# Second attention of a two-layer Flamingo block: transposed scores, row maxima from a first pass, fp32 value products

## The chip, the cores and the metric

One core of a Trainium2 chip runs the whole program: one launch, all inputs in HBM at the start, the output in HBM at the end. The metric is device time in microseconds; lower is better. A core has five engines that run their own programs and wait for each other through semaphores: TensorE (PE, matmuls into PSUM), VectorE (DVE), ScalarE (ACT), GpSimd (POOL) and SyncE (SP), which here only starts DMAs.

## What is computed

X (4 batches, 512 positions, 512 features) goes through two layers, each a cross attention and a feed-forward net, each added to X with a gate. The fourth of five stages is the attention of the second layer, and the change is there:

```python
def xattn(q, k, v):              # 4 batches, width 512 split into 8 heads of 64 rows (ch = 64)
    attn = einsum('bct,bcs->bts', q * ch**-0.5, k * ch**-0.5)   # per head 512 x 512
    attn = softmax(attn, axis=-1)
    return einsum('bts,bcs->bct', attn, v)
# q = layernorm(X), k = v = ctx_2048; X += tanh(g_xattn[1]) * result
```

The width is the second axis of X (512 rows, 64 of them a head), and the queries t and the keys s are its last axis. So in memory a head is 64 partitions, two heads make a tile of 128, and queries and keys are its 512 columns.

## The kernel before

The program has five stages one after the other, with a barrier between: `mlstm_phase`, `spline_phase`, `ffn0_phase`, `attention_phase`, `ffn1_phase`. Each stage is written as one program for each engine; the order on an engine is the order of the code, and every `wait_ge` blocks all that stands behind it on the same engine. No planner is at work.

`attention_phase` goes through the 4 batches. At the start of a batch (`norm`, `split`) VectorE takes the maximum of ctx, GpSimd spreads it over partitions (L1770), VectorE normalises X into XN and ScalarE and VectorE split keys, queries and values into a high and a low fp16 part (KH/KL, QH/QL, VH/VL), so that three fp16 products stand for one fp32 product. TensorE turns ctx for the values (L1868).

Then come 32 units in a row, one for each head (8) and each block of 128 queries (4). A unit is:

- `scores` (L1832): three fp16 matmuls, 128 queries by 512 keys, into one of three PSUM banks. The keys of a head stand in 128 rows of which 64 are zero, so that all 128 rows of the array are used.
- `top` (L1944, L1946): VectorE takes the row maximum, negates and scales it.
- exponential (L1805): ScalarE with that as bias, and with the row sum as a second output.
- `turn` (L1840): four fp32 transposes of the probabilities, 128 x 128 each.
- `high`, `low` (L1792, L1950): ScalarE and VectorE split the turned probabilities into fp16 parts.
- `weigh` (L1852): twelve fp16 matmuls of 64 columns.
- `scale` (L1798): ScalarE multiplies by the inverse sum (L1955) into OT.

Every eighth unit `back` turns a finished block (L1860) and VectorE adds it into X (L1960). TensorE's order in the loop is scores of unit u + 2, turn of u, weigh of u - 2. The three pairs of weights of the next stage (W1H, W1L) are loaded here by SyncE, one pair at each of the first three batches (L1749).

`ffn1_phase` runs 16 tiles of 128 rows; the gate and up products of a tile (L2084) use W index 0 and 1, the down products (L2110) index 2, and they begin two tiles later.

Of the kernel before, what the change touches and what calls it, by code (L numbers as in the profile page):

```python
# [1699 lines left out]

def attention_phase(nc, A, X, tg, idf, store, WH1, WL1, stack):


    def sb(name, shape, dt=F32):
# [21 lines left out]
    RS = sb("RS2", [P, NC])  # L1726
    EPS = sb("EPS2", [P, 1])
    CM = sb("CM2", [P, 8])
    SB = [stack.enter_context(nc.psum_tensor(f"A_S{i}", [P, 512], F32)) for i in range(3)]
    PB = [stack.enter_context(nc.psum_tensor(f"A_P{i}", [P, 512], F32)) for i in range(2)]  # L1730
    OB = [stack.enter_context(nc.psum_tensor(f"A_O{i}", [P, 512], F32)) for i in range(2)]
    TB = stack.enter_context(nc.psum_tensor("A_T", [P, 512], F32))
    (ctx_loaded, mv_ready, sd_ready, xn_ready, t_ready, t_taken, s_ready, max_ready, p_ready, pt_ready, ph_ready,
     pl_ready, o_ready, ot_ready, own_sem, passed, pre_ready, cm_ready, cm_all, cs_ready, vh_ready,
     vl_ready, kh_ready, kl_ready, qh_ready, ql_ready, rc_ready, norm_own) = (sem("d_" + n) for n in (
         "ctx", "mv", "sd", "xn", "t", "t_taken", "s", "max", "p", "pt", "ph", "pl", "o", "ot", "own", "passed", "pre", "cm", "cm_all", "cs", "vh", "vl", "kh", "kl", "qh", "ql", "rc", "norm_own"))
# [606 lines left out]
```

## Time and profile before

| what | value |
|---|---|
| median of 3 runs | 1674.55 us (1672.92 to 1677.72) |
| profiled execution, own time | 1677.74 us |
| its span | 1676.0 us |
| mean granted clock of TensorE | 0.901 |
| TensorE busy | 1346.0 us |
| VectorE busy | 1241.5 us |
| ScalarE busy | 767.8 us |
| GpSimd busy | 325.5 us |

Busy time is the union of an engine's instructions. The span is that of one profiled execution; its own time lies 1.7 us above. A matmul's length in a row covers its way through the array, so that the distance of two starts, and not the length, is what one costs in a stream. The granted clock is a share of full speed: 1.0 is 2.4 GHz and 0.5 is 1.2 GHz; a mean between the two is a mixture of both.

### The profile page before, as it was taken

The numbers are of one execution on the slowest core, as the hardware profiler recorded it, in microseconds if no ns is written. First come the engines' busy times: TensorE is split into PE (matmuls) and PEld (weight loads), VectorE is DVE, ScalarE is ACT, GpSimd is POOL, SyncE is SP. The second block draws the span as 40 slices with busy tenths as digits, with TensorE's granted clock in tenths as the row PEclk, the third lists the DMA queues.
The fourth block names the chain that finished last, engine by engine and source line by source line (L and its number), as shares of the span: only waits on it lengthen the run. The fifth ranks groups of instructions, "written<-read, shape, count | busy, mean of one in ns | idle before, by whom it ended". The sixth has DMA issues, their size and how long they took to land. (4 is left out here: it accounts for less than half of the span.)

```text
span 1676.0 us, 24635 instructions
## 1 busy us (share of the span) xinstructions
PE 1346.0 (80%) x8976; PEld 758.8 (45%) x9000; DVE 1241.5 (74%) x1952; ACT 767.8 (46%) x1451; POOL 325.5 (19%) x233
## 2 busy tenths in 40 slices
PE   5599993636868989873967759679999999999996
PEld 3378773212334444432645546334444444444443
DVE  5567777825558778956999999488877777887764
ACT  3445562715334444424978879323333334433322
POOL 0032424607445557531000000000000000000000
PEclk8789996558888999996979889789999999999998
DMA  8312231355142242226030000000000000000000
GB/s 290 117 52 61 102 101 41 128 147 157 55 131 83 90 124 88 101 67 247 3 125 0 25 0 0 1 1 7 6 6 13 6 6 6 6 6 9 10 6 13
DMA packets 56493, 102.17 MB, mean 61 GB/s; under 512 B 9823, under 2 KB 20727, under 8 KB 56300
## 3 DMA queue, kind: packets, MB, share of 16 engines
q1 hardware_dynamic: 55148, 97.14, 17.5%
q0 software_dynamic: 1280, 4.20, 0.9%
q8 instruction: 37, 0.61, 0.2%
q14 instruction: 28, 0.23, 0.0%
HBM read 73.47 MB, written 27.66 MB: 60 GB/s over the span
## 5 line engine op out<-in xcount | busy, mean ns | idle before, releaser
L2084 PE MATMUL HG<-W1H,XT 128*128 128x512 f16 x512 | 166.6, 387 | 27.2 <-ACT XT L2045 20.7
L1558 PE MATMUL FD<-W0D,HH 128*128 128x512 f16 x512 | 159.6, 395 | 14.8 <-DMA W0D<-down_weights,IDX 12.2
L2084 PE MATMUL HU<-W1H,XT 128*128 128x512 f16 x512 | 163.2, 380 | 0.0
L2110 PE MATMUL HD<-W1H,HT 128*128 128x512 f16 x512 | 155.2, 380 | 0.0
L1552 PE MATMUL FG<-F,W0G 97*128 97x512 f16 x324 | 86.1, 400 | 52.9 <-DMA F<-features_kept 24.5
L2053 ACT ACTIVATE SG<-HG,DS 128x512 f32<-128x512 f32 x64 | 43.9, 686 | 160.6 <-PE HU L2084 160.6
L1805 ACT ACTIVATE PR<-A_S,NM,CM 128x512 f32<-128x512 f32 x128 | 99.5, 777 | 34.2 <-DVE NM L1946 34.2
L2187 DVE SCALAR_TENSOR_TENSOR H<-HU,DS,SG 128x512 f32<-128x512 f32 x64 | 48.0, 750 | 87.6 <-ACT SG L2053 85.7
L1442 POOL TENSOR_TENSOR HL<-HM,HH 128x512 f16<-128x512 f32 x64 | 92.3, 1442 | 86.0 <-ACT HH L1481 85.5
L335 ACT ACTIVATE DD<-E,TM 128x128 f32<-128x128 f32 x256 | 72.7, 369 | 70.3 <-PE E L431 68.7
L1558 PE MATMUL FD<-W0D,HL 128*128 128x512 f16 x256 | 100.1, 391 | 0.0
L2084 PE MATMUL HG<-W1L,XT 128*128 128x512 f16 x256 | 99.1, 387 | 0.0
L2110 PE MATMUL HD<-W1L,HT 128*128 128x512 f16 x256 | 97.2, 380 | 0.0
L2084 PE MATMUL HU<-W1L,XT 128*128 128x512 f16 x256 | 97.2, 380 | 0.0
L1481 ACT CAST HH<-HM 128x512 f16<-128x512 f32 x64 | 39.6, 618 | 120.4 <-DVE HM L1645 120.4
L1944 DVE TENSOR_REDUCE NM<-A_S 128x1 f32<-128x512 f32 x128 | 86.3, 674 | 8.3 <-PE A_S L1832 8.3
L1832 PE MATMUL A_S<-KH,QH 128*128 128x512 f16 x128 | 52.1, 407 | 49.9 <-DVE VL L1939 49.9
L2084 PEld LDWEIGHTS HG<-W1H,XT 128*128 128x128 f16 x512 | 50.8, 99 | 91.2 <-DVE H L2187 27.7
L1950 DVE SCALAR_TENSOR_TENSOR PL<-A_P,PH 128x512 f16<-128x512 f32 x128 | 87.9, 686 | 5.2 <-ACT PH L1792 4.8
L2062 ACT CAST HQ<-V 128x2048 f16<-128x2048 f32 x16 | 30.4, 1898 | 128.4 <-DVEq L2209 128.4
L1840 PE MATMUL A_P<-CST,PR 128*128 128x128 f32 x512 | 83.2, 286 | 6.9 <-ACT PR L1805 6.3
L1645 DVE SCALAR_TENSOR_TENSOR HM<-FG,DS,SG 128x512 f32<-128x512 f32 x54 | 40.5, 750 | 64.5 <-PE FG L1552 35.4
(335 smaller groups left out, 3369.8 us busy)
## 6 DMA issues: line engine op xcount, KB each, us to landing
VALP<-in_ffn_weights_dram SPq DMA_DIRECT2D x24, 512.0 KB, 3.6
VALQ<-in_ffn_weights_dram SPq DMA_DIRECT2D x24, 512.0 KB, 3.6
quantised_weights<-QQ SPq DMA_DIRECT2D x24, 512.0 KB, 2.8
X<-in_x_dram SPq DMA_DIRECT2D x8, 1024.0 KB, 6.0
CTX<-in_ctx_dram SPq DMA_DIRECT2D x8, 1024.0 KB, 5.6
W1H<-quantised_weights SPq DMA_DIRECT2D x3, 2048.0 KB, 10.6
W1L<-quantised_weights SPq DMA_DIRECT2D x3, 2048.0 KB, 15.4
F<-features_kept SPq DMA_DIRECT2D x16, 288.0 KB
```

What stands on the lines that cost most here:

```text
L335: ins = nc.scalar.activation(DD[:, n % 4, c * P:(c + 1) * P], E[n % 2][:, c * P:(c + 1) * P], ACT.Exp, bias=TM[:, 13 + c, b, h:h + 1])
L1442: pool.tensor_tensor(HL[:, i, :], HM[:, i % 2, :], HH[:, i, :], ALU.subtract).then_inc(hl_ready, 1)
L1552: last = pe.matmul(banks[t][:, :], GW[rows, t, lhs, cols], F[b % 2][rows, rhs, c, :], start=(n == 0), stop=(n == 2))
L1558: last = pe.matmul(DN[c][:, :], lhs[:, i, c * P:(c + 1) * P], W2[:, i, part, :], start=(i == 0 and n == 0), stop=(i == KI - 1 and n == 2))
L1805: nc.scalar.activation(PR[:, u % 2, :], SB[u % 3][:, :], ACT.Exp, bias=NM[:, 1, u:u + 1], scale=CM[:, 5:6], accum_out=SM[:, u:u + 1]).then ...
L1832: last = pe.matmul(SB[u % 3][:, :], lhs[:, c, cols], rhs[:, c, par, :], start=(i == 0), stop=(i == 2))
L1840: last = pe.transpose(PB[u % 2][:, k * P:(k + 1) * P], PR[:, u % 2, k * P:(k + 1) * P], idf)
L1944: own.inc(v.tensor_reduce(NM[:, 0, u:u + 1], SB[u % 3][:, :], AX.X, ALU.max, negate=True))
L1950: v.scalar_tensor_tensor(out=PL[:, u % 3, :], in0=PB[u % 2][:, :], scalar=XS, in1=PH[:, u % 3, :], op0=ALU.mult, op1=ALU.subtract).then_in ...
L2084: ins = pe.matmul(bank[:, :], lhs, rhs, start=(i == 0), stop=(i == len(terms) - 1))
L2110: ins = pe.matmul(DN[0][:, :], HT[:, q, lp, k, :], W[:, 2, i * D:(i + 1) * D], start=(i == 0 and lp == 0 and W is WH), stop=(i == KI - 1 a ...
L2187: v.scalar_tensor_tensor(out=H[:, i * 512:(i + 1) * 512], in0=U[i % 2][:, :], scalar=DS[:, 1:2], in1=SG[:, i % 2, :], op0=ALU.mult, op1=AL ...
```

## The change

The whole of `attention_phase` is written anew; the loops over batches are unrolled.

- A step is now two heads (the two halves of 128 partitions), one block of 128 keys, and all 512 queries: 64 steps, `STEPS_A`. Eight steps (two pairs of heads) are a quad. The scores come out transposed, keys in partitions, so the turn of the probabilities, their split and the turn back of the result are gone.
- `scores(k)`: six fp16 matmuls with 64 contraction rows (two heads, in different halves of the array's rows, into different PSUM banks), and one more for each head with two contraction rows, a row of ones against the negated maxima of the queries (`MB`, as a bf16 pair).
- These maxima come from a first pass one quad ahead: `largest(g, i)` multiplies only the high parts, 128 queries by 512 keys for two heads, into the one buffer `MX`; VectorE's `slot(g, i)` reduces it with one instruction. Eight slots make a quad. `negatives` splits them and TensorE transposes them; ScalarE copies them to `MB`. `SLOTS` says in which step each is issued.
- One exponential for 128 x 1024 values, without a bias and without sums.
- `weigh(k)`: value products in fp32, two matmuls of 64 array columns and 512 moving columns, accumulated over the four key blocks in `OB`. The values are kept in fp32 only (`VT`).
- The sums of the probabilities: GpSimd adds the four key blocks of a head (two additions of 128x512 in each step but the first of four), TensorE adds over partitions with ones (`sums`), VectorE takes the reciprocal of the 128x512 result (`inverse_sums`), TensorE spreads it over the rows of the heads with the gate in it (`spread`), VectorE multiplies (`normalise`) and GpSimd adds to X (`residual`). This runs for quad g - 1 while quad g is computed.
- The split of the next batch is spread over the steps of even quads. Queries are normalised on ScalarE and their low part is made on GpSimd; K2 has no zero rows, so the two memsets L1765 and L1766 are gone.
- ctx, XN, the values and the queries stand in the room of the weights W1H and W1L. Weights index 0 are loaded at the second batch, index 1 when the last batch is split, and index 2 at the start of `ffn1_phase`.

```diff
+STEPS_A = B * NC * NC
+QUADS = STEPS_A // 8
+RING = 6
+SLOTS = ((0, 1), (2,), (3,), (4, 5), (6,), (7,), (), ())
...
+    MX = stack.enter_context(nc.psum_tensor("A_M", [P, 2, S], F32))
+    SB = [stack.enter_context(nc.psum_tensor(f"A_S{i}", [P, 2, S], F32)) for i in range(2)]
+    OB = stack.enter_context(nc.psum_tensor("A_O", [P, S], F32))
+    TB = stack.enter_context(nc.psum_tensor("A_T", [P, S], F32))
...
+    for k in range(STEPS_A):
+        g, step = divmod(k, 8)
+        j = k % NC
+        pool.wait_ge(p_ready, k + 1)
+        if j and step == j and g:
+            pool.wait_ge(all_ready, g)
+        for par in range(2):
+            s = SS[:, 2 * (step // NC) + par, :]
+            if j == 1:
+                pool.wait_ge(p_ready, k + 1)
+                ins = pool.tensor_tensor(s, PT[:, (k - 1) % RING, par, :], PT[:, k % RING, par, :], ALU.add)
...
+        if step == 7:
+            if g:
+                residual(g - 1)
+            if g % 2 == 0 and g // 2 + 1 < B:
+                low(g // 2 + 1)
+    residual(QUADS - 1)
...
+    for k in range(STEPS_A):
+        g, step = divmod(k, 8)
+        b = g // 2 + 1
+        act.wait_ge(s_ready, k + 1)
+        if k >= RING:
+            act.wait_ge(o_ready, k - RING + 1)
+            done = k - RING if (k - RING) % NC else k - RING + 1
+            act.wait_ge(added, done - done // NC)
+        nc.scalar.activation(PT[:, k % RING, :, :], SB[k % 2][:, :, :], ACT.Exp,
+                             scale=CM[:, (g // 2) % 2, 5:6]).then_inc(p_ready, 1)
+        if k % NC == 0 and k:
+            unscaled(k // NC - 1)
+        if g % 2 == 0 and b < B:
+            first = 3 if g == 0 else 0
+            if first <= step < first + NC:
+                values(b, step - first, TB[:, :])
+            if step == 2:
+                deviation(b)
+            if step in (4, 5):
+                keys(b, slice(2 * (step - 4), 2 * (step - 4) + 2))
+            if step == 6:
+                queries(b)
+            if step == 7:
+                high(b)
+        if step == 7 and g + 1 < QUADS:
+            negated(g + 1)
...
+    def largest(g, i):
+        b, c, q = g // 2, 2 * (g % 2) + i // NC, i % NC
+        pe.wait_ge(qh_ready, b + 1)
+        pe.wait_ge(kh_ready, b + 1)
+        if g or i:
+            pe.wait_ge(mx_taken, 8 * g + i)
+        if i == 0 and g:
+            pe.wait_ge(mb_ready, g)
...
+        for par, r in enumerate(half):
+            last = pe.matmul(MX[:, par, :], Q2[r, b % 2, 0, c, q * P:(q + 1) * P], K2[r, b % 2, 0, c, :],
+                             start=True, stop=True)
+        last.then_inc(mx_ready, 1)
...
+    def scores(k):
+        g, step = divmod(k, 8)
+        b, c, j = g // 2, 2 * (g % 2) + step // NC, k % NC
+        cols = slice(j * P, (j + 1) * P)
+        if step == 0:
+            pe.wait_ge(mb_ready, g + 1)
+            pe.wait_ge(kl_ready, b + 1)
+            pe.wait_ge(ql_ready, b + 1)
+        if k >= 2:
+            pe.wait_ge(p_ready, k - 1)
+        bank = SB[k % 2]
+        for i, (kp, qp) in enumerate(((0, 0), (1, 0), (0, 1))):
+            for par, r in enumerate(half):
+                pe.matmul(bank[:, par, :], K2[r, b % 2, kp, c, cols], Q2[r, b % 2, qp, c, :], start=(i == 0), stop=False)
+        for par in range(2):
+            row = 32 * (2 * (step // NC) + par)
+            last = pe.matmul(bank[:, par, :], ONES[row:row + 2, :], MB[row:row + 2, g % 2, :], start=False, stop=True)
+        last.then_inc(s_ready, 1)
...
+        for par, r in enumerate(half):
+            last = pe.matmul(OB[r, :], VT[:, b % 2, j, c * P + par * AC:c * P + (par + 1) * AC],
+                             PT[:, k % RING, par, :], start=(j == 0), stop=(j == NC - 1))
+        last.then_inc(o_ready, 1)
...
+    def sums(g):
+        pe.wait_ge(sum_ready, 4 * (g + 1))
+        if g:
+            pe.wait_ge(rep_taken, 2 * g)
+        for i in range(4):
+            last = pe.matmul(TB[32 * i:32 * i + 32, :], ONE[:, :], SS[:, i, :], start=True, stop=True)
+        last.then_inc(all_ready, 1)
+    def spread(g, q):
+        pe.wait_ge(r_ready, g + 1)
+        if q:
+            pe.wait_ge(rep_taken, 2 * g + 1)
+        pe.matmul(TB[:, :], PAIR[:, q, :], R4[:, :], start=True, stop=True).then_inc(rep_ready, 1)
...
+    for k in range(STEPS_A):
+        g, step = divmod(k, 8)
+        b = g // 2 + 1
+        if step == 7:
+            weigh(k)
+        if k + 1 < STEPS_A:
+            scores(k + 1)
+        if g + 1 < QUADS:
+            for i in SLOTS[step]:
+                largest(g + 1, i)
+        if g % 2 == 0 and b < B:
+            j = step - (3 if g == 0 else 0)
+            if 0 <= j < NC:
+                if j:
+                    pe.wait_ge(vt_ready, NC * b + j)
+                elif g:
+                    pe.wait_ge(rep_taken, 2 * (g - 1))
+                turn(b, j, TB)
+        if g and step >= 6:
+            spread(g - 1, step - 6)
+        if step < 7:
+            weigh(k)
+        if g and step == 4:
+            if g % 2 == 0 and b < B:
+                pe.wait_ge(vt_ready, NC * (b + 1))
+            sums(g - 1)
+        if step == 6 and g + 1 < QUADS:
+            negatives(g + 1)
...
+    def slot(g, i):
+        v.wait_ge(mx_ready, 8 * g + i + 1)
+        if i == 0 and g:
+            v.wait_ge(np_ready, g)
+        at = 2 * (i // NC)
+        v.tensor_reduce(NQ[:, i % NC, at:at + 2], MX[:, :, :], AX.X, ALU.max, negate=True).then_inc(mx_taken, 1)
...
+    def inverse_sums(g):
+        v.wait_ge(all_ready, g + 1)
+        if g:
+            v.wait_ge(rep_ready, 2 * g)
+        v.reciprocal(R4[:, :], TB[:, :]).then_inc(r_ready, 1)
+    def normalise(g, q):
+        v.wait_ge(rep_ready, 2 * g + q + 1)
+        v.wait_ge(o_taken, 2 * g + q + 1)
+        o = OS[:, g % 2, q, :]
+        v.tensor_tensor(o, o, TB[:, :], ALU.mult).then_inc(rep_taken, 1)
...
+    for g in range(QUADS):
+        b = g // 2 + 1
+        prep = g % 2 == 0 and b < B
+        more = g + 1 < QUADS
+        if prep and g:
+            top(b)
+        if more:
+            slot(g + 1, 0)
+            slot(g + 1, 1)
+        if prep:
+            statistics(b)
+        if more:
+            slot(g + 1, 2)
+        if prep:
+            if g == 0:
+                top(b)
+            inverse(b)
+        if more:
+            slot(g + 1, 3)
+        if prep:
+            scale(b)
+        if more:
+            slot(g + 1, 4)
+            slot(g + 1, 5)
+        if g:
+            inverse_sums(g - 1)
+        if more:
+            slot(g + 1, 6)
+        if prep:
+            low(b)
+        if more:
+            slot(g + 1, 7)
+            negatives(g + 1)
+        if g:
+            normalise(g - 1, 0)
+            normalise(g - 1, 1)
+    inverse_sums(QUADS - 1)
...
+    for part, W in enumerate((WH, WL)):
+        sp.dma_start(W[:, 2, :].rearrange("p (q c) -> p q c", c=QT),
+                     store[2 * QTILES:3 * QTILES, part].rearrange("q p c -> p q c")).then_inc(down_loaded, 16)
...
+        pe.wait_ge(down_loaded, 32)
```

## Rows read from the trace of the kernel before

**Rows 1.** the page, part 1: busy time and share of the span, instructions

```profile
PE 1346.0 (80%) x8976; PEld 758.8 (45%) x9000; DVE 1241.5 (74%) x1952; ACT 767.8 (46%) x1451; POOL 325.5 (19%) x233
```

**Rows 2.** busy time by stretch (columns: stretch, us, engines with counts, clock, DMA)

```profile
752.00:783.00 31.00, 3.68 (x16) 3.28 (x16) 17.42 (x29) 11.08 (x10) 7.26 (x3) 0.59 0.57 202
...
836.00:857.00 21.00, 4.96 (x60) 3.84 (x59) 19.63 (x32) 12.75 (x16) 0.35 (x1) 0.67 0.19 59
857.00:910.00 53.00, 51.06 (x596) 34.70 (x594) 48.98 (x130) 47.94 (x125) 0.00 (x0) 0.97 0.20 76
```

**Rows 3.** timeline in the second batch, steady units (start, length, engine, line)

```profile
882.55 0.38 PE L1832 MATMUL A_S<-KL,QH 128*128 128x512 f16 x1
...
882.76 0.38 PE L1832 MATMUL A_S<-KH,QL 128*128 128x512 f16 x1
...
882.97 0.67 DVE L1944 TENSOR_REDUCE NM<-A_S 128x1 f32<-128x512 f32 x1
...
883.68 0.21 DVE L1946 TENSOR_SCALAR NM<-NM,CM 128x1 f32<-128x1 f32 x1
...
883.81 0.69 DVE L1950 SCALAR_TENSOR_TENSOR PL<-A_P,PH 128x512 f16<-128x512 f32 x1
...
884.42 0.15 DVE L1955 RECIPROCAL RC<-SM 128x1 f32<-128x1 f32 x1
884.49 0.67 DVE L1944 TENSOR_REDUCE NM<-A_S 128x1 f32<-128x512 f32 x1
```

**Rows 4.** timeline of TensorE in the first stage: fp32 calls, small row tiles

```profile
53.96 3.60 PE L381 MATMUL O<-KT,WG 128*32 128x512 f32 x16
58.41 1.11 PE L391 MATMUL O<-ZALL,CST 128*112 128x512 f32 x2 [0.85 <-ACT ZALL L285]
...
144.00 0.38 PE L431 MATMUL E<-NP,PICK 96*128 96x512 bf16 x1
144.31 1.16 PE L411 MATMUL QK<-X,KT 32*128 32x128 f32 x16
145.40 0.86 PE L442 MATMUL O<-VA,CC 128*128 128x33 f32 x6
```

**Rows 5.** groups by shape, VectorE (busy us, mean ns | idle before)

```profile
L1204 DVE TENSOR_REDUCE AMQ<-VALP 128x32 f32<-128x1024 f32 x24 | 29.2, 1215 | 15.2 <-DMA VALP<-in_ffn_weights_dram 15.1
...
L2201 DVE RECIPROCAL HI<-HA 128x64 f32<-128x64 f32 x16 | 8.9, 553 | 0.6
...
L1305 DVE RECIPROCAL IVQ<-AMQ 128x32 f32<-128x32 f32 x24 | 8.4, 348 | 23.7 <-DMA VALQ<-in_ffn_weights_dram 22.3
```

**Rows 6.** groups by shape, ScalarE

```profile
L2059 ACT COPY HT<-HT 128x1024 f16<-128x1024 f16 x64 | 60.0, 1027 | 3.7 <-PE HT L2102 3.7
...
L1783 ACT CAST QH<-XN 128x2048 f16<-128x2048 f32 x4 | 7.6, 1898 | 0.1
```

**Rows 7.** the line L1442 on GpSimd (ns min/median/max)

```profile
L1442 POOL TENSOR_TENSOR HL<-HM,HH x64: 1142/1415/2327, 377.9 to 691.9; 128x512 f16<-128x512 f32 x64
```

**Rows 8.** timeline at the start and the end of the stage

```profile
757.56 2.82 PE L1868 MATMUL A_S<-CST,CTX 128*128 128x128 f32 x12 [6.71 <-DMA CTX<-in_ctx_dram]
758.92 2.29 DVE L1895 TENSOR_REDUCE CM<-CTX 128x1 f32<-128x2048 f32 x1 [6.87 <-POOL KL L1766]
...
770.03 0.38 POOL L1770 PARTITION_ALL_REDUCE CM<-CM  x1 [11.14 <-issue]
...
783.24 0.61 PE L1832 MATMUL A_S<-KH,QH 128*128 128x512 f16 x1 [22.00 <-DVE VL L1939]
...
1058.99 0.75 DVE L1960 SCALAR_TENSOR_TENSOR X<-A_T,CM,X 128x512 f32<-128x512 f32 x1 [1.75 <-PE A_T L1860]
```

**Rows 9.** the page, part 6: DMA issues, KB each, us to landing

```profile
W1L<-quantised_weights SPq DMA_DIRECT2D x3, 2048.0 KB, 15.4
```

**Rows 10.** third stage: TensorE's timeline, and the stretch after it

```profile
714.00 1.87 PE L1351 MATMUL FT<-IDH,QQ 128*128 128x128 f16 x16 [2.89 <-POOL QQ L1335]
...
714.80:718.20 3.40, 3.40 (x20) 1.94 (x19) 3.15 (x5) 1.93 (x2) 0.41 (x1) 0.71 0.63 189
```

More of the change, by code:

```diff
@@ L1726, in attention_phase @@
     RS = sb("RS2", [P, NC])
+    NB = sb("NB2", [P, NC])
     EPS = sb("EPS2", [P, 1])
[L1728 to L1736, printed above, removed]
@@ L1761, in _ @@
-            sp.wait_ge(w_loaded, 16 * 6)
+            for b in range(B):
+                if b:
+                    sp.wait_ge(kl_ready, b)
+                    sp.wait_ge(vt_turned, NC * b)
+                sp.dma_start(CTX[:, :, :], ctx[b]).then_inc(ctx_in[b], 16)
+                if b == 1:
+                    weights(0)
+            sp.wait_ge(kl_ready, B)
+            sp.wait_ge(vt_turned, NC * B)
+            sp.wait_ge(ql_ready, B)
+            weights(1)
+            sp.wait_ge(w_loaded, 16 * 4)
@@ new lines, in low, with residual @@
+            def low(b):
+                pool.wait_ge(qh_ready, b + 1)
+                pool.wait_ge(xn_ready, b + 1)
+                pool.tensor_tensor(Q2[:, b % 2, 1, :, :], XN[:, :, :], Q2[:, b % 2, 0, :, :], ALU.subtract).then_inc(ql_ready, 1)
+            def residual(g):
+                for q in range(2):
+                    c = 2 * g + q
+                    pool.wait_ge(rep_taken, c + 1)
+                    x = X[:, c, :]
+                    pool.tensor_tensor(x, x, OS[:, g % 2, q, :], ALU.add).then_inc(x_added, 1)
@@ L1817, in _, with queries @@
-            split(0)
-            with act.Fori(0, B - 1) as b:
-                batch(b, True)
-            batch(B - 1, False)
+                ins = nc.scalar.activation(K2[:, b % 2, 0, cs, :], CTX[:, cs, :], ACT.Copy, scale=CM[:, b % 2, 4:5])
+                if cs.stop == NC:
+                    ins.then_inc(kh_ready, 1)
+            def queries(b):
+                act.wait_ge(rs_ready, b + 1)
+                for c in range(NC):
+                    ins = nc.scalar.activation(XN[:, c, :], X[:, b * NC + c, :], ACT.Identity, scale=RS[:, c:c + 1],
+                                               bias=NB[:, c:c + 1])
+                ins.then_inc(xn_ready, 1)
@@ new lines, in _ @@
+            act.wait_ge(consts, CONSTS + 1)
+            deviation(0)
+            queries(0)
+            high(0)
+            for j in range(NC):
+                values(0, j, SB[j // 2][:, j % 2, :])
+            keys(0, slice(0, NC))
+            negated(0)
+            for k in range(STEPS_A):
[24 more added lines that the diff above has]
+                    negated(g + 1)
@@ new lines, in turn @@
+            def turn(b, j, bank):
+                pe.wait_ge(ctx_in[b], 16)
+                for c in range(NC):
+                    last = pe.transpose(bank[:, c * P:(c + 1) * P], CTX[:, c, j * P:(j + 1) * P], idf)
+                last.then_inc(vt_turned, 1)
+            def largest(g, i):
[10 more added lines that the diff above has]
+                last.then_inc(mx_ready, 1)
@@ L1887, in _ @@
+            sums(QUADS - 1)
+            for q in range(2):
+                spread(QUADS - 1, q)
         @block.vector
         def _(v):
-            v.memset(EPS[:, :], 1e-5).then_inc(pre_ready, 1)
-            v.sem_inc(t_taken, 1)
-            v.wait_ge(pre_ready, 3)
-            def norm(b):
-                own = Tally(v, norm_own, b, OWN_NORM)
-                v.wait_ge(ctx_loaded, b * 16 + 16)
-                v.tensor_reduce(CM[:, 0:1], CTX[:, :, :].rearrange("p c d -> p (c d)"), AX.X, ALU.max,
+            n_own = [0]
```

353 lines of the change are left out of this document (155 added, 198 removed).

## The prediction, made before the result was known

> **What bounds the kernel now.** I read the page first, then the busy time by stretch, the timeline of a few units, and last the rows of other stages that resemble the new instructions. The page's shares (TensorE 80%, VectorE 74%, GpSimd 19%) are averages over five stages and say nothing about this one [rows 1]. The stretches do: the second attention begins at 752.0 and ends at 1059.7 with the last addition into X, so it takes 308 us of 1676 [rows 2, 8]. It is four times the same: about 53 us of dense units and, before each, 21 to 31 us in which TensorE is busy for only 4 to 5 us because keys, queries and values of the batch are being split [rows 2]. In the dense part 32 units take 48.6 us at the steady pace: one row-maximum to the next is 1.52 us [rows 3]. In it VectorE has 0.67 + 0.21 + 0.69 + 0.15 of overlapping work and TensorE hardly less (busy 51.1 of 53 us), ScalarE 47.9 [rows 2, 3]. So three engines are level, the batch starts leave holes, and GpSimd is empty.
>
> **The change on TensorE.** A step is now two heads by 128 keys by all 512 queries; 64 steps in 8 quads of 8. An fp16 matmul of 512 columns starts every 0.215 us [rows 3]. An fp32 call of 512 columns is two records; where calls go to different column tiles two records run in one interval: 16 records in 3.60 us, less the last one's 0.59 length, are 7 intervals of 0.43 [rows 4]. Alone, two records take 1.11 [rows 4]. The row tiles pair too: 16 records of 128 columns start within 0.9 us, where one after the other they would need twice that [rows 4]. So a step costs 3 x 0.215 for the six score matmuls, 0.22 for the two mask rows, 0.22 for the two of "largest" (when there is one) and 2 x 0.43 for the fp32 value products.
>
> Between them the array's tile shape changes: 64 rows, 32 rows, 64 rows, 64 columns, 64 rows. The trace has this at the 32-row scores: their first matmul starts 0.31 after the 512-column one before it instead of 0.215, and the way back to a full tile also lies beyond the stream [rows 4]. That is 0.1 of drain each way, and 0.1 more where the weight load behind it is uncovered; I take 0.17, bounds 0 (these shapes may not count as different) and 0.25. The Trainium skill, "TensorEngine Tiling (Array Packing)", Key Properties, says that changing the tiling mode, not only the tile, drains the engine; by that rule every one of these borders pays and the sum stays as it is below, while if only full against partial tiles paid, it would be some 40 less. The row agrees with it for full against 32 rows; no run here shows 64 against 32.
>
> A step is then 2.63 with "largest" (four switches) and 2.24 without (three). A quad has six of the one, two of the other, and two extra "largest": 20.7. To it come the sums (four fp32 calls in four column tiles, 0.9 to 1.7, I take 1.3 and a switch: 1.5), two spreads (2 x 1.06), and four fp32 transposes (0.65): 25.0. Even quads that prepare a batch add 16 transposes: a dozen took 2.82 at half clock [rows 8], so 0.12 each at full clock, with switches 3.0.
>
> **The waits that it adds.** There is one MX buffer, so each "largest" waits for the VectorE reduction of the one before. A reduction of 1024 columns takes 1.22 [rows 5]. In steps 0 and 3 two stand back to back in TensorE's program: 0.17 of tail, 1.22 and two hand-overs make 1.5 each, with the weigh of the step and all scores behind it queued. The third is worse. VectorE has the reciprocal of the 128x512 sums between slots 5 and 6. Reciprocal costs 0.348 for 32 and 0.553 for 64 columns, 6.4 ns a column [rows 5]: 3.4 us for 512 (bounds 0.7, an ordinary pass such as L1950's, and 3.5). It starts when TensorE has done the sums at the end of step 4; the "largest" of step 5 needs slot 6, which is behind it: 0.2 + 3.4 + 1.2 + 0.1 = 5.0 after the sums, when TensorE arrives at 1.2. That is 3.8 us of stall in each of quads 1 to 6. Together 6.8, a quad is 31.8. VectorE's batch work (a 2.3 reduction, four statistics, the fp16 rest) stands between slots and adds about 2 more in quads 2 and 4.
>
> Quad 0 has no sums, spreads or reciprocal: 31.8 - 1.5 - 2.1 - 3.8 + 3.0 + 0.5 = 27.9. Quads 1, 3, 5, 6: 127.2. Quads 2, 4: 2 x (31.8 + 3 + 2) = 73.6. Up to quad 7: 228.7; its first five steps and the sums of quad 6: 12.7.
>
> **What stays covered.** ScalarE: an exponential over 1024 columns is near the 1.03 of a 1024-column copy, say 1.1 [rows 6]; with the copies of values (four), keys, queries and high parts (1.9) of a batch it has about 2.1 a step, under 3.9. GpSimd: an fp32 addition over 512 columns is bounded by 1.14 and 2.33 [rows 7]; I take 1.2, since what VectorE runs beside it here reads PSUM. 14 a quad, and four times as much work in a low part, 4.6, are 17 to 21, under 31.8. Its additions of step 1 wait for the sums of the quad before, so it works a burst behind, which the six PT buffers cover: exponential 6 needs the addition of step 1, 2.4 after the sums, during TensorE's 3.8 stall. The down weights now load at the start of the last stage: the longer pair-half takes 15.4 us to landing, two in a row are bounded by 31 [rows 9], while one of its 16 tiles takes (1676 - 1060)/16 = 38 us and the first down product comes after two tiles; 0. If that cover went, it would cost those 31. The loads of index 0 and 1 start in quads 0 and 4 and end before quad 7.
>
> **Start and end.** ctx lands at 757.6 as before [rows 8]. The 7 us of memsets on GpSimd go, so the maximum of ctx can start 1.3 earlier. The all-reduce came 8.8 after that maximum [rows 8]; I keep it (bound 5). Then scales at 770, keys (128x2048 in one, 1.9 by the cast [rows 6]) at 772, and before slot 0 VectorE's low part, 2.3: 774.4. Eight slots alternate between TensorE at half clock (0.64) and VectorE (1.22), 1.96 each: 789.4; negation, transposes and copy: 792.1. First scores came at 783.2 before. So 40.1, and 3 for half clock in the first steps (before: from 783.2 to 788). The end is GpSimd's: after the sums of quad 6 it has six steps of additions to do, 14.4, while TensorE needs 8; then sums 1.9 (half clock), reciprocal 3.5, spread 1.9, product 0.75, again 1.9 and 0.75, residual 1.2, hand-overs 1: 27.3.
>
> **The clock.** After a gap of 2.9 us with only transposes following, the granted clock in the following stretch is 0.71, and matmuls that had 0.215 intervals took twice that [rows 10]: about 1.7 us lost. A stall of 3.8 is longer than that. Six times 1.7 is 10 (bounds 0 and 30). The Trainium skill, "TensorE: Matmul & The Clock Gate", Why this matters for your kernels, says that idle gaps between matmul bursts bring the half clock back; the row agrees, and by that rule these stalls pay as I have it, while without it the sum would be 10 less.
>
> Sum: 40.1 + 3 + 228.7 + 12.7 + 27.3 + 10 = 321.8 against 307.7: 14 us more. Against the profiled execution (span 1676.0, own time 1677.7) that is a span of 1690; the median shown, 1674.55, lies 3.2 below that execution, so **1689**.
>
> **Rivals.** (a) Forecast: the work is smaller, but waits, start and end return it: 1675 to 1705, chance 0.45. (b) Faster: the tile switches cost nothing, or nearly. 30 a quad are 240; at 0 instead of 0.17 the sum falls by 41, of which the stall of step 5 takes a few back: 284, 1650. It decides at 0.11 a switch, where the stage breaks even. For it: only full against 32 rows is measured. Against: that row is regular. A cheaper reciprocal goes the same way: at 0.7 us it saves 2.7 in seven quads, 19 us, 1669. Chance together 0.3, of which some lands near 1670. (c) The tiles pair less well: fp32 value products of 64 columns take three or four intervals instead of two: + 0.43 or 0.86 x 64, 1716 or 1744; the fp16 pairs in series + 1.09 x 64, 1759. Against it stand both rows of pairs, but with 32-wide tiles. Chance 0.12. (d) The clock stays at half much longer, since each quad has three gaps: mean 0.8 over 200 us of work adds 40 instead of 10: 1719. Chance 0.09. (e) GpSimd is the bound: at 2.2 an addition it has 35 a quad, + 30: 1719. The Trainium skill, "SBUF — State Buffer", Who interferes with whom, says that GpSimd is blocked by VectorE operations with two SBUF inputs and not by tensor_reduce; L1442's spread agrees with a blocking by neighbours. By that rule only three low parts could block here. Chance 0.04.
>
> Within 0.3% (5 us, about what a measurement of this kernel can tell) 0.12: the edges of (a) and (b). Faster 0.33, slower 0.55. The range must reach to (b)'s 1650 with some of its cheaper reciprocal, and to (d) and the first of (c): 1643 to 1730. The forecast's own is 1675 to 1705.
>
> **What would show it.** First scores (of the second pass) near 792; steps of 2.2 to 2.6 us; TensorE idle before "largest" on VectorE's reduction, about 1.5 us twice a quad and 3.8 once, behind a reciprocal of 3.4; half-clock stretches after it; an end of 27 us in which TensorE idles on GpSimd. Wrong would be: exponentials spaced by ScalarE's own 1.1 to 2 us (stage near 250), value products at 0.86 a record pair in series, a reciprocal under 1 us, or GpSimd additions near 2 us with TensorE waiting on them.

## The result

The changed kernel takes 1707.4 us (median of four runs, 1704.1 to 1717.4) against 1673.7 for the kernel before beside it: ratio 1.0196, 95% interval 1.0172 to 1.0219. That is 33.7 us slower, where 14 were forecast (1689). The spans of the profiled executions differ by 28.6 (1704.6 against 1676.0).

The page, part 1, of the changed kernel answers to [rows 1]:

```profile
PE 1360.1 (80%) x7528; PEld 664.8 (39%) x7528; DVE 1133.7 (67%) x1497; ACT 658.1 (39%) x1042; POOL 480.9 (28%) x355
```

VectorE and ScalarE work 108 and 110 us less, GpSimd 155 more, and TensorE, with 1448 matmul records fewer, 14 us more. The busy time by stretch shows where (columns as in [rows 2]; the cuts are the start, the quads 0, 1, 2 and 6, each from its first scores to the next quad's, and quad 7 with the end):

```profile
750.20:790.60 40.40, 9.66 (x38) 5.11 (x40) 22.49 (x31) 10.94 (x14) 5.98 (x10) 0.56 0.43 156
790.60:824.40 33.80, 26.05 (x132) 7.32 (x132) 19.40 (x29) 22.54 (x25) 12.10 (x9) 0.86 0.09 32
824.40:856.10 31.70, 25.27 (x126) 6.11 (x127) 15.69 (x13) 10.47 (x11) 21.40 (x16) 0.89 0.00 1
856.10:899.90 43.80, 33.88 (x146) 9.49 (x146) 24.60 (x32) 22.05 (x25) 19.24 (x16) 0.77 0.08 25
...
1012.20:1046.40 34.20, 27.80 (x132) 6.52 (x132) 16.16 (x14) 10.56 (x11) 17.43 (x15) 0.85 0.01 1
1046.40:1089.00 42.60, 26.85 (x124) 6.34 (x122) 10.15 (x7) 10.35 (x11) 26.36 (x22) 0.77 0.00 1
```

The stage takes 338.8 us, 31.1 more than before, and 17 more than the sum of the prediction. The last stage, which now loads the down weights itself, takes 615.6 us against 616.2 before, so that load is covered, as forecast. No engine is busy throughout: in quad 6 TensorE works 27.8 of 34.2 us, at a mean granted clock of 0.85, where the dense units before had 0.97 [rows 2]. Quads 2 and 4, which prepare a batch, take 44.

A piece of the timeline of quad 5, odd like quad 6 and with the same course, shows both losses:

```profile
983.03 0.39 PE L1927 MATMUL A_M<-K,W1L 64*128 64x512 f16 x2 [1.41 <-DVE NQ L2085]
...
983.36 1.25 PE L1965 MATMUL A_O<-PT,W1H 128*64 128x512 f32 x4
983.46 1.22 DVE L2085 TENSOR_REDUCE NQ<-A_M 128x2 f32<-128x1024 f32 x1 [0.58 <-PE A_M L1927]
...
984.54 1.46 PE L1950 MATMUL A_S<-W1L,K 64*128 64x512 f16 x6
...
987.01 1.97 PE L1965 MATMUL A_O<-PT,W1H 128*64 128x512 f32 x4
...
991.21 1.08 PE L1965 MATMUL A_O<-PT,W1H 128*64 128x512 f32 x4
...
992.22 0.82 PE L1950 MATMUL A_S<-W1L,K 64*128 64x512 f16 x6
...
995.09 0.39 PE L1927 MATMUL A_M<-K,W1L 64*128 64x512 f16 x2 [1.41 <-DVE NQ L2085]
...
995.42 1.08 PE L1965 MATMUL A_O<-PT,W1H 128*64 128x512 f32 x4
...
996.43 0.82 PE L1950 MATMUL A_S<-W1L,K 64*128 64x512 f16 x6
...
998.83 1.06 PE L1974 MATMUL A_T<-SS,ONE 128*32 128x512 f32 x8
...
999.96 3.36 DVE L2103 RECIPROCAL R<-A_T 128x512 f32<-128x512 f32 x1 [3.21 <-PE A_T L1974]
...
1003.24 1.16 DVE L2085 TENSOR_REDUCE NQ<-A_M 128x2 f32<-128x1024 f32 x1
...
1004.54 0.59 PE L1927 MATMUL A_M<-K,W1L 64*128 64x512 f16 x2 [3.58 <-DVE NQ L2085]
...
1005.06 1.97 PE L1965 MATMUL A_O<-PT,W1H 128*64 128x512 f32 x4
```

In the rows W1H stands for ctx, XN and the values, and W1L for the queries, which lie in the room of these weights. Read it from below. At 1004.54 the eighth `largest` has waited 3.58 us for VectorE: the sums end at 999.9, the reciprocal takes 3.36, the seventh reduction stands behind it, and only then is MX free. The value product after it takes 1.97 instead of 1.08: the clock has gone from 2.4 to 1.2 GHz. The same is at 983.03: a second `largest` of a step waits 1.41, and the scores at 984.54 and the products at 987.01 run at half clock (1.46 and 1.97), until at 991.21 and 992.22 they are back at 1.08 and 0.82. So a short pause can be followed by half clock too. It isn't always: behind the same wait of 1.41 at 995.09 everything stays at full clock (1.08 at 995.42, 0.82 at 996.43). In quads 1, 3, 5 and 6 four of the eight waits of 1.41 are followed by half clock, and in quads 1 to 6 all six of 3.58; the waits of 1.43 and 3.32 in quad 0 are not. What makes the difference no run here shows.

The start, in the timeline (answers to the first rows of [rows 8]):

```profile
755.35 2.29 DVE L2039 TENSOR_REDUCE CM<-W1H 128x1 f32<-128x2048 f32 x1 [1.94 <-DMA W1H<-in_ctx_dram]
...
758.65 0.38 POOL L1788 PARTITION_ALL_REDUCE CM<-CM  x1 [6.66 <-issue]
...
761.12 1.90 ACT L1858 CAST W1L<-W1H 128x2048 f16<-128x2048 f32 x1
...
764.83 2.03 ACT L1845 ACTIVATE K<-W1H,CM 128x2048 f16<-128x2048 f32 x1
...
766.66 4.05 POOL L1793 TENSOR_TENSOR W1L<-W1H,W1L 128x2048 f16<-128x2048 f32 x1 [7.63 <-issue]
766.97 5.88 DVE L2077 SCALAR_TENSOR_TENSOR K<-W1H,CM,K 128x2048 f16<-128x2048 f32 x1 [7.13 <-ACT K L1845]
772.78 1.21 DVE L2085 TENSOR_REDUCE NQ<-A_M 128x2 f32<-128x1024 f32 x1
...
774.78 1.23 DVE L2085 TENSOR_REDUCE NQ<-A_M 128x2 f32<-128x1024 f32 x1 [0.79 <-PE A_M L1927]
...
790.58 1.46 PE L1950 MATMUL A_S<-W1L,K 64*128 64x512 f16 x6 [0.72 <-issue]
```

And the end (answers to its last row):

```profile
1058.92 1.07 PE L1974 MATMUL A_T<-SS,ONE 128*32 128x512 f32 x8
...
1076.49 1.94 PE L1974 MATMUL A_T<-SS,ONE 128*32 128x512 f32 x8 [8.97 <-POOL SS L1818]
...
1078.50 3.36 DVE L2103 RECIPROCAL R<-A_T 128x512 f32<-128x512 f32 x1 [10.25 <-PE A_T L1974]
...
1087.70 1.26 POOL L1800 TENSOR_TENSOR X<-X,OS 128x512 f32<-128x512 f32 x1 [1.65 <-DVE OS L2109]
```

Groups by line over the stage, of VectorE, ScalarE, TensorE and GpSimd, answer to the bounds in [rows 5 to 7]:

```profile
L2085 DVE TENSOR_REDUCE NQ<-A_M 128x2 f32<-128x1024 f32 x64 | 77.8, 1216 | 57.3 <-PE A_M L1927 57.3
L2103 DVE RECIPROCAL R<-A_T 128x512 f32<-128x512 f32 x8 | 26.9, 3358 | 47.1 <-PE A_T L1974 47.1
...
L1890 ACT ACTIVATE PT<-A_S,CM 128x1024 f32<-128x1024 f32 x64 | 71.2, 1114 | 104.0 <-PE A_S L1953 77.9 <-POOLq L1827 26.0
...
L1927 PE MATMUL A_M<-K,W1L 64*128 64x512 f16 x128 | 30.0, 459 | 72.1 <-DVE NQ L2085 64.1 <-ACT K L1845 8.0
...
L1818 POOL TENSOR_TENSOR SS<-SS,PT 128x512 f32<-128x512 f32 x64 | 84.9, 1348 | 8.3 <-POOL SS L1815 4.1 <-POOL SS L1818 4.0 <-ACT PT L1890 0.2
...
L1800 POOL TENSOR_TENSOR X<-X,OS 128x512 f32<-128x512 f32 x16 | 19.9, 1263 | 8.6 <-DVE OS L2109 7.5 <-POOL SS L1818 1.1
```

TensorE waits 64.1 us ahead of `largest` for VectorE's reductions (49.2 of it in quads 0 to 6, the rest in the start). ScalarE waits 26.0 us for GpSimd; whether that costs anything the groups can't say, since it may lie beside TensorE's own waits.

### The profile page after: what moved, and what is told of

Read it like the earlier page. It is cut to its first block and busy times, and to the rows that moved or that the text cites. A ratio compares the mean times of both kernels' runs of the same rounds, so it can differ in the third digit from the quotient of the medians.

```text
span 1704.6 us, 20241 instructions
## 1 busy us (share of the span) xinstructions
PE 1360.1 (80%) x7528; PEld 664.8 (39%) x7528; DVE 1133.7 (67%) x1497; ACT 658.1 (39%) x1042; POOL 480.9 (28%) x355
## 5 line engine op out<-in xcount | busy, mean ns | idle before, releaser
L1558 PE MATMUL FD<-W0D,HH 128*128 128x512 f16 x512 | 158.4, 392 | 15.1 <-DMA W0D<-down_weights,IDX 11.4
L1442 POOL TENSOR_TENSOR HL<-HM,HH 128x512 f16<-128x512 f32 x64 | 92.6, 1447 | 83.0 <-ACT HH L1481 82.8
L2085 DVE TENSOR_REDUCE NQ<-A_M 128x2 f32<-128x1024 f32 x64 | 77.8, 1216 | 57.3 <-PE A_M L1927 57.3
L1890 ACT ACTIVATE PT<-A_S,CM 128x1024 f32<-128x1024 f32 x64 | 71.2, 1114 | 104.0 <-PE A_S L1953 77.9
L1927 PE MATMUL A_M<-K,W1L 64*128 64x512 f16 x128 | 30.0, 459 | 72.1 <-DVE NQ L2085 64.1
L1818 POOL TENSOR_TENSOR SS<-SS,PT 128x512 f32<-128x512 f32 x64 | 84.9, 1348 | 8.3 <-POOL SS L1815 4.1
L2266 PEld LDWEIGHTS HG<-W1H,XT 128*128 128x128 f16 x512 | 50.8, 99 | 91.2 <-DVE H L2370 27.8
L1965 PE MATMUL A_O<-PT,W1H 128*64 128x512 f32 x256 | 84.5, 746 | 0.1
L1645 DVE SCALAR_TENSOR_TENSOR HM<-FG,DS,SG 128x512 f32<-128x512 f32 x54 | 40.5, 749 | 61.6 <-PE FG L1552 33.8
```

Source lines behind the costliest of these rows:

```text
L1442: pool.tensor_tensor(HL[:, i, :], HM[:, i % 2, :], HH[:, i, :], ALU.subtract).then_inc(hl_ready, 1)
L1558: last = pe.matmul(DN[c][:, :], lhs[:, i, c * P:(c + 1) * P], W2[:, i, part, :], start=(i == 0 and n == 0), stop=(i == KI - 1 and n == 2))
L1818: ins = pool.tensor_tensor(s, s, PT[:, k % RING, par, :], ALU.add)
L1890: nc.scalar.activation(PT[:, k % RING, :, :], SB[k % 2][:, :, :], ACT.Exp, scale=CM[:, (g // 2) % 2, 5:6]).then_inc(p_ready, 1)
L1965: last = pe.matmul(OB[r, :], VT[:, b % 2, j, c * P + par * AC:c * P + (par + 1) * AC], PT[:, k % RING, par, :], start=(j == 0), stop=(j == ...
L2085: v.tensor_reduce(NQ[:, i % NC, at:at + 2], MX[:, :, :], AX.X, ALU.max, negate=True).then_inc(mx_taken, 1)
```

## Experiments

Theory W: TensorE's waits behind VectorE, and the half clock that follows each, carry the loss. Rival P: TensorE's own work bounds the quads. Rival G: GpSimd's additions do. All runs but the combined ones are the changed kernel with one edit. In the table "stage" is from the last addition of the stage before to the last addition of this one (308.1 in the kernel before), "quads" is from the first scores to those of quad 7, "half" the time in it that the trace's record of the granted clock gives at 1.2 GHz, and "wait" TensorE's waits ahead of `largest` for VectorE in it (us, one profiled execution each). Waits ahead of the negatives' transposes are not in it. Medians and ratios to the kernel before are of the timed runs, four to ten for each version; the kernel before had 1673.7 to 1677.2 beside them, so differences of medians between two rows are good to a few us. The profiled execution can lie well off the median (1685.3 against 1676.6 for copy_for_reciprocal), and the stages ahead of this one, which no edit touches, end 748.4 to 755.3 us after the start. So where the two differ, "stage" is the better measure of an edit.

| kernel | median | ratio, 95% interval | stage | quads | half | wait |
|---|---|---|---|---|---|---|
| changed | 1707.4 | 1.0196, 1.0172 to 1.0219 | 339.0 | 255.8 | 88 | 49.2 |
| copy_for_reciprocal | 1676.6 | 1.0014, 0.9990 to 1.0038 | 315.5 | 235.8 | 72 | 33.2 |
| reciprocal_behind_slot6 | 1678.6 | 1.0022, 1.0002 to 1.0042 | 316.9 | 234.2 | 69 | 27.6 |
| second_after_weigh | 1684.7 | 1.0061, 1.0043 to 1.0080 | 318.5 | 235.9 | 64 | 40.7 |
| inverse_behind_slot5 | 1700.1 | 1.0151, 1.0133 to 1.0170 | 332.4 | 249.8 | 85 | 44.3 |
| fill_the_stall | 1691.7 | 1.0107, 1.0068 to 1.0145 | 323.4 | 241.0 | 51 | 27.6 |
| fill_every_wait | 1681.0 | 1.0026, 1.0011 to 1.0042 | 312.1 | 229.3 | 7 | 7.1 |
| two_sum_buffers | 1704.5 | 1.0163, 1.0116 to 1.0209 | 335.9 | 262.1 | 107 | 48.3 |
| no_mask_rows | 1674.9 | 1.0001, 0.9986 to 1.0016 | 308.4 | 227.2 | 66 | 53.3 |
| mask_in_64_rows | 1688.9 | 1.0074, 1.0053 to 1.0096 | 323.5 | 241.1 | 74 | 50.7 |
| combined_prep | 1649.4 | 0.9820, 0.9776 to 0.9864 | 280.0 | 206.9 | 38 | 13.1 |
| combined_one_set | 1664.6 | 0.9922, 0.9893 to 0.9951 | 296.8 | 214.3 | 41 | 15.0 |
| combined_fill | 1642.6 | 0.9794, 0.9766 to 0.9821 | 274.2 | 201.4 | 14 | 13.8 |
| combined_64 | 1639.1 | 0.9777, 0.9744 to 0.9809 | 270.2 | 197.0 | 3 | 18.1 |

**The reciprocal, made cheap, and moved.**

```diff
-                v.reciprocal(R4[:, :], TB[:, :]).then_inc(r_ready, 1)
+                v.tensor_copy(R4[:, :], TB[:, :]).then_inc(r_ready, 1)
```

> The reciprocal of the sums (3.36 us in the changed kernel, seven in the quads and one in the tail) becomes a copy of the same 512 columns, so the output is not divided by the sums; nothing else changes. Theory W (TensorE's waits behind VectorE and the half clock that follows each): the wait of 3.58 us ahead of the eighth `largest` falls to about 0.8 in the six quads 1 to 6, 6 x 2.8 = 17 us, 2.8 more in the tail, and with it goes a half-clock stretch of 3.4 to 6.8 us a quad, worth half of its length, 1.7 to 3.4: in all 29 to 39 us faster than the changed kernel. Without the clock's part: 20 faster. Rival P (TensorE's own work bounds the quads): 20 at most, no change of the clock. Rival G (GpSimd's additions bound them): only the tail's 3 us, and ScalarE's waits for GpSimd grow by what TensorE's shrink.

30.8 us faster by the medians, W's range; but the stage is only 23.6 shorter, under that range and just above the 20 without the clock's part. The wait ahead of the eighth `largest` fell to 0.86 to 0.96. Waits fell by 16.0, the end by 2.7 and half clock by 16 us, worth 5 by the 0.33 a us measured below: 24 in all. So the clock has a part in it, but a smaller one than W's 10 to 20: none of the eighth `largest` is followed by half clock any more, yet six of the eight waits of 1.41 in quads 1, 3, 5 and 6 now are, where four were. The order alone does nearly as much:

```diff
-                if g:
-                    inverse_sums(g - 1)
                 if more:
                     slot(g + 1, 6)
+                if g:
+                    inverse_sums(g - 1)
```

> Only VectorE's order changes: the reciprocal of the sums (3.36 us) comes behind the reduction of the seventh tile, not ahead of it, so that the eighth `largest` no longer stands behind it; the eighth reduction and the row-maximum work then come 3.4 us later, beside a step of TensorE's. Theory W: of the wait of 3.58 us a quad some 0.8 is left ahead of the transposes of the negatives in odd quads and about 3 in quads 2, 4 and 6, where `low` of the next batch (2.6 us) or nothing else lies between them: 12 to 17 us direct and 5 to 10 by half clock less, 15 to 25 us faster than the changed kernel. Rival P: 0 to 5, the wait only moves to the negatives.

28.8 us faster by the medians, above my range, and 22.1 by the stage, inside it; P had 0 to 5. The same reciprocal now runs beside a step of TensorE's. The waits ahead of `largest` fell by 21.6, of which 8.4 came back ahead of the negatives' transposes (3.3 to 11.7), and half clock fell by 19. Quads 1, 3, 5 and 6 took 25.3 to 33.2 us, but quad 0 rose from 33.8 to 38.6.

**The pairs of `largest`.**

```diff
-                    for i in SLOTS[step]:
+                    for i in SLOTS[step][:1]:
                         largest(g + 1, i)
...
                 if step < 7:
                     weigh(k)
+                if g + 1 < QUADS:
+                    for i in SLOTS[step][1:]:
+                        largest(g + 1, i)
```

> In the steps that issue two `largest`, the second is issued behind the step's value product (1.08 us) instead of straight behind the first, so that TensorE has work while VectorE reduces the first. Theory W: of the two waits of 1.41 us in each of seven quads about 1.1 goes, 14 x 1.1 = 15 us, and more if the half clock behind them goes too: 14 to 25 us faster than the changed kernel. Rival P: the waits go and the time does not, because ScalarE's exponential is what the next scores wait for: 0 to 5 faster. Rival G: 0 to 5 faster, with longer waits of ScalarE for GpSimd.

22.7 us faster (the stage 20.6), as W says, though not as it sums it: waits fell by only 8.5 of the 15, half clock by 24 us.

**The batch's statistics.** `inverse(b)` moved from behind `slot(g + 1, 2)` to behind `slot(g + 1, 5)`.

> Only VectorE's order in the three quads that prepare a batch changes: the inverse deviations, which wait for ScalarE's square root, come behind the sixth reduction instead of ahead of the fourth. Theory W: the wait of 2.11 us ahead of step 3's first `largest` goes in quads 2 and 4 and its like in quad 0, and some half clock with it: 4 to 10 us faster than the changed kernel. Rival P or G: within 2 us of it.

7.3 faster (the stage 6.6): VectorE's wait for ScalarE's square root was one of the pauses of the even quads.

**The clock by itself.** The next two shorten no wait and only give TensorE something to do in it (the second also waits, ahead of a fill into TB, until TB is free).

```diff
                     for i in SLOTS[step]:
+                        if g and i == 7:
+                            for _ in range(16):
+                                pe.matmul(OB[:, :], ZERO[:, :], K2[:, (g // 2) % 2, 0, 0, :], start=False, stop=False)
                         largest(g + 1, i)
```

> Sixteen matmuls of a zero weight tile over 512 fp16 columns (16 x 0.215 = 3.4 us at full clock) are added into the open accumulation ahead of the eighth `largest` of quads 1 to 7, which waits 3.58 us for VectorE there; they change no value. If the half clock behind that wait comes of TensorE's pause, as theory W has it, the half-clock stretches behind it (3.4 to 6.8 us a quad, half of that each) go: 10 to 20 us faster than the changed kernel, less about 1 us where the fill is longer than the wait. If the clock does not hang on the pause: 0 to 8 slower (the fill at half clock takes 6.9 us in a wait of 3.6).

15.7 faster, and the same by the stage. So the half clock hangs on the pause, and matmuls of zeros hold it off. With all pauses filled (5 ahead of the second tile, 11 in quads 2 and 4; 3 or 9 ahead of the fourth in even quads; 6 ahead of the sixth; 16 ahead of the eighth; 15 ahead of quad 0's transposes):

> The fill of zero-weight matmuls stands ahead of every wait for VectorE over 0.8 us in the changed kernel's quads (5 to 16 of them, as long as each wait is at full clock); no value changes and no wait is shortened. It measures the clock's share of the changed kernel's loss. Theory W: the fill ahead of the eighth tile took half-clock time in the quads from 87.7 us to 50.6 and 14.8 us off the stage, 0.40 a us; with all waits filled some 10 to 30 us at half clock are left, mostly of the start: 22 to 31 us faster than the changed kernel. If the half clock comes of something other than the pauses of the quads (its own work, or the start): no more than the 15 us of the one fill.

26.4 us faster, 26.9 by the stage, inside W's range. In the busy time by stretch of quads 0 to 6 the clock is 0.98; of the changed kernel first, then of this one:

```profile
790.60:1046.40 255.80, 202.59 (x932) 51.77 (x934) 132.80 (x148) 108.81 (x119) 131.63 (x97) 0.83 0.07 25
```

```profile
795.60:1024.90 229.30, 218.63 (x1153) 66.43 (x1155) 133.16 (x148) 108.59 (x119) 130.49 (x96) 0.98 0.08 28
```

TensorE is busier by 16 us, with 47 us or more of nothing added, and the quads are 26.5 shorter: the clock's loss in them, 0.33 us for each of the 81 us at half clock that went. The 7 us that are left are those of the first steps, where the half clock of the start lasts on.

**GpSimd.** `SS` with eight buffers, index `4 * (g % 2) + ...`, and GpSimd's wait for the sums one quad later.

> The partial sums get a second set of four buffers, so that GpSimd no longer waits for TensorE's sums of the quad before it adds the next one's. Theory W: ScalarE's waits for GpSimd (26.0 us in 7 places) go, but most of them lie beside TensorE's waits for VectorE, so the quads gain 0 to 8 us and the tail some 7 us, by which GpSimd is late at the end: 7 to 15 us faster than the changed kernel. Rival G: the 26 us and the tail's 7, 33 us faster.

3 us faster, within the spread of four runs each (the intervals overlap), and 3.1 by the stage. The group of the exponentials has lost its wait for GpSimd, 26.0 us, and waits for the scores instead:

```profile
L1890 ACT ACTIVATE PT<-A_S,CM 128x1024 f32<-128x1024 f32 x64 | 71.3, 1114 | 108.7 <-PE A_S L1953 108.7
```

So rival G is out for the changed kernel's quads: those waits lay beside others. The end gained 9 us as the additions came earlier (quad 7 and the end 33.6 instead of 42.6), and the quads gave 6 back with more half clock (107 us against 88) at the same waits. Why there was more of it, I didn't find.

**TensorE's own work.** The `ONES`/`MB` matmuls are left out.

> The two matmuls per step that add the negative row maximum as contraction rows (2 rows, bf16; 128 in all) are left out, so the exponentials are taken without the maximum's shift; everything else stays. Theory W: each step loses one interval of 0.215 us and two switches of about 0.1 us at full clock and twice as much at half clock, 64 x 0.42 to 0.55 = 27 to 35 us of TensorE's work, of which the part beside waits is not gained: 12 to 25 us faster than the changed kernel. Rival P (its own work alone bounds the quads): 27 to 35 faster. Rival G: 0 to 5.

32.5 faster (the stage 30.6): P's figure, not W's. A steady step of the last quad went from 2.08 to 1.76 us, and all of it counts. With the prices below, 22 such steps are 7.0 and the 42 with `largest`, at 0.42 each, 17.6; 21 us less at half clock are 7.0 more: 31.6. So W and P are not alternatives here: TensorE's work and its waits stand in series, and either one shortens the stage. What a change of tile shape costs, the next run asks; the ones sit in two rows of a 64-row weight, zero elsewhere, and `slot` writes the pair's columns two apart:

```diff
-                    row = 32 * (2 * (step // NC) + par)
-                    last = pe.matmul(bank[:, par, :], ONES[row:row + 2, :], MB[row:row + 2, g % 2, :], start=False, stop=True)
+                    r = half[par]
+                    last = pe.matmul(bank[:, par, :], ONES[r, step // NC, :], MB[r, g % 2, :], start=False, stop=True)
```

> The changed kernel with the mask matmuls in row tiles of 64 rows, like the scores ahead of them, instead of 32: the ones stand in two rows of a 64-row weight that is zero elsewhere, one half of the array for each head; same count, same columns, same values. It prices the switches. If only a change of the tile's shape costs, and the trace's 0.1 us is the price of one, step 6's last quad goes from steps of 2.09 us to 1.99, 64 x 0.1 = 6 us, 4 to 9 us faster than the changed kernel. If the small price seen was the price of the 32-row tile both ways: up to 13 faster. If a switch costs nothing and 2.09 has another cause: within 2.

18.5 faster, 15.5 by the stage, beyond all three figures. TensorE's timeline, first of the changed kernel, a step without `largest`:

```profile
1052.68 0.82 PE L1950 MATMUL A_S<-W1L,K 64*128 64x512 f16 x6
1053.43 0.39 PE L1953 MATMUL A_S<-MB,ONES 2*128 2x512 bf16 x2
1053.75 1.08 PE L1965 MATMUL A_O<-PT,W1H 128*64 128x512 f32 x4
1054.76 0.82 PE L1950 MATMUL A_S<-W1L,K 64*128 64x512 f16 x6
```

and of this kernel, a step with it:

```profile
980.70 0.82 PE L1954 MATMUL A_S<-W1L,K 64*128 64x512 f16 x6
981.36 0.38 PE L1957 MATMUL A_S<-MB,ONES 64*128 64x512 bf16 x2
981.58 0.38 PE L1931 MATMUL A_M<-K,W1L 64*128 64x512 f16 x2
981.89 1.08 PE L1969 MATMUL A_O<-PT,W1H 128*64 128x512 f32 x4
982.90 0.82 PE L1954 MATMUL A_S<-W1L,K 64*128 64x512 f16 x6
```

From scores to mask rows it is 0.75 with the 32-row tile and 0.66 with the 64-row one (three intervals of 0.215 are 0.65); from mask rows to `largest` 0.32 and 0.22; from any of them to the value products 0.31 to 0.32. One border is 0.1 us. The steps say 0.11 to 0.12 on average: 2.08 is 0.36 above its 1.72 of work, with three borders, and 2.40 is 0.46 above 1.94, with four. I had counted one border a step; where `largest` follows, two go: such a step is 2.20 against 2.40 (the 32-row tile, where TensorE doesn't wait). Over 42 of them at 0.2 and 22 steps at 0.1 that is 10.6, and 14 us less at half clock by the 0.33 above are 4.5: 15.1, where the stage, from first scores to last addition, became 15.3 shorter.

**Together.** combined_prep is second_after_weigh, reciprocal_behind_slot6, inverse_behind_slot5 and two_sum_buffers; combined_one_set leaves the last out.

> Four edits together: the second `largest` of a step behind its value product, the reciprocal behind the seventh reduction, the inverse deviations behind the sixth, and two sets of sum buffers. Theory W: most of TensorE's waits for VectorE go (72 us of wait ahead of `largest`, 8 of them from elsewhere, to about 25), half-clock time in the quads falls from 88 us to under 50, and GpSimd, which would be next, has its second buffers: 45 to 60 us faster than the changed kernel, 12 to 27 faster than the kernel before. Rival P: 20 faster than the changed kernel. Rival G: no faster than the best single edit so far, 22.

> The combined version without the second set of sum buffers. It tells how much GpSimd bounds once TensorE's waits are shorter; alone the second set gave 2.6 us of the stage. Rival G in its weak form (GpSimd is next in line): 12 to 20 us slower than the combined version, with ScalarE's waits for GpSimd back at 20 us or more and the tail 8 us longer. Theory W taken alone: only the tail's 9 us, as the tail was 41.4 with one set and 32.4 with two.

The four edits give 58 us, and the kernel is 1.8% faster than the one before. Without the second set 15.2 of it is lost, 16.8 by the stage: 9.0 in the end, where W alone had them too, and 7.5 in the quads, with 25.0 us of ScalarE's waits for GpSimd. So once TensorE waits less, the weak form of G holds. combined_fill adds twelve matmuls of zeros ahead of the negatives' transposes in quads 0, 2 and 4; combined_64 the 64-row mask as well, and its zero weights have 32 columns instead of 128.

> The combined version with twelve zero-weight matmuls (2.6 us at full clock) ahead of the transposes of the negatives in quads 0, 2 and 4, where its pauses of 2.8 to 3.4 us are the longest left in the quads. Theory W: half-clock time of 37.7 us in quads 0 to 6 falls to about 20 and 4 to 9 us come off; if the clock is held down by the start alone, within 2 us of the combined version.

> The combined version with its fill and the mask rows in 64-row tiles. If a switch is 0.1 us: 5 to 9 us faster than the combined version with its fill, as its quads have few waits left to hide it; if nothing: within 2 of it.

6.8 and 3.5 more by the medians, 5.8 and 4.0 by the stage; the intervals of the ratios overlap, so neither step is clear of the spread by the medians alone. The last is under my 5 to 9: its quads are 4.4 shorter, and TensorE's waits for VectorE have grown from 13.8 to 18.1 us. Its busy time by stretch, quads 0 to 6:

```profile
790.80:987.80 197.00, 166.07 (x966) 51.19 (x966) 133.50 (x148) 108.22 (x119) 136.09 (x100) 0.99 0.10 33
```

It is the best version found: 1639.1 us, 2.2% faster than the kernel before (1677.2 beside it; interval 1.9 to 2.6%), its quads at full clock nearly throughout.

## Why the prediction was right in sign and wrong in size

- **Start.** Forecast 40.1 to the first scores, measured 40.4, by another way: the all-reduce came 1.0 after the maximum, not 8.8, so the scales were there at 759.8 and not at 770. But ScalarE first cast the queries and copied the values, so that its keys ended at 766.9, 7.1 after the scales, where I had 2, and VectorE's low part took 5.9 beside GpSimd's, where I had 2.3. These errors cancel, by luck.
- **Waits.** 1.5, 1.5 and 3.8 a quad were forecast, 1.41, 1.41 and 3.58 measured, the reciprocal 3.36 against 3.4. The mechanism is shown by the reciprocal's copy, its move, and the moved `largest`: each shortened the stage by 20 to 24 us.
- **Clock: the step that failed.** "Six times 1.7 is 10 (bounds 0 and 30)", with 3 for the first steps: 13. Measured by filling the pauses of quads 0 to 6: 26.5. The mechanism was right, the size was not: I let only the longest wait of a quad cost clock and put the others at nothing without a reason. By the 0.33 above, the half clock behind the six waits of 3.58 (31 us) is worth 10 and that of the first steps (9 us) 3, both as forecast. The rest of the 88 us is what I left out: 21 us behind four of the eight waits of 1.41 in quads 1, 3, 5 and 6, and 27 us in quads 2 and 4 behind waits of 2.80 and of 2.11 with 1.42 close behind, 48 us worth 16. Each stretch lasted 3.4 to 10 us. Rival (d) had the mechanism, at 40 in place of 10; with the first steps that is 43, and the 26.5 lies about halfway.
- **TensorE's work.** With the clock's loss taken out, fill_every_wait's quads come to 229.3 against 228.7 forecast, which looks better than it is. Quads 1, 3, 5 and 6 are 28.5 to 29.6, not 31.8: the steps take 2.40 and 2.08 instead of 2.63 and 2.24, 1.7 less in a quad, the sums 1.0 instead of 1.5, and the waits 6.4 instead of 6.8. Quad 0 is 34.6, not 27.9, and quads 2 and 4 are 38.8, not 36.8: VectorE's batch work between the slots, its wait for ScalarE's root, and the negatives' wait (3.32 in quad 0) were undercounted. So this sum too came out by luck. A border from 64 to 32 rows costs 0.1, and where both matmuls have 64-row tiles there is nothing; so the trace agrees with the Trainium skill, "TensorEngine Tiling (Array Packing)", Key Properties, that a change of tiling mode drains the engine.
- **Rival (b)** fell on the price it names: it decides at 0.11 a switch, and the steps show 0.11 to 0.12. It gave some 13 us, and the clock took it. **Rival (c)** is refuted: four records of the value products take 1.08, two intervals. **Rival (e)** is refuted as it stands: GpSimd's additions took 1.26 to 1.35 on average, not 2.2, and two_sum_buffers shows that they don't bound the quads; in the combined kernel one set of sum buffers costs 7.5 us in the quads.
- **End.** Quad 7 and the end: 42.6 against 40.0; its additions are 1.25 each, where I had 1.2, and GpSimd is last.

In sum, against the 321.8 forecast for the stage: start 0.3, work 0.6, clock 13.5, end 2.6, together 17.0. What stays open: the timed medians differ by 33.7, the spans of the two profiled executions by 28.6; why four waits of 1.41 were followed by half clock and four were not; and the extra half clock of two_sum_buffers.

## What to carry to other kernels

With one buffer between two engines, ask of every instruction on the consumer what stands in front of the release: moving one reciprocal behind one reduction shortened the stage by 22 us here, with the reciprocal as long as before. Price each pause of TensorE twice, its length and the half clock behind it, and fill one to measure the second. When an engine's work and its waits are in series, both experiments "win", and only the sum tells the bound.

## What the hardware showed that I had not expected

- Half of the pauses of 1.4 us in quads 1, 3, 5 and 6 were followed by half clock, and matmuls with zero weights in the pauses kept it away: 88 us at half clock in quads 0 to 6 became 7.
- Fp32 calls in four column tiles run side by side: the eight records of the sums took 1.06 us, as long as four in two tiles (1.08).
- VectorE's pass over 128x2048 with two SBUF inputs took 5.88 us beside GpSimd's subtraction (4.05 us), where the mean of all four, this one included, is 3.69.
- The first all-reduce (0.38 us) began 1.0 us after the maximum that it reads had ended, where in the kernel before it was 8.8 [rows 8]. GpSimd's low part then began 3.6 us after the cast of the queries that it waits for (761.12 and 1.90). The profile shows no reason for either.
